# A perceiver block on one core: q turned through DRAM and by VectorE instead of by TensorE

## The reference, cut to what matters

```python
x = x + xattn(layernorm(x), ctx, ctx, 0, mask)   # 32 query heads of 32, 8 groups of keys (4 heads share one)
x = x + s4(layernorm(x))                         # along the 1024 features: a causal convolution with a kernel K, + D*u
x = x + ffn(layernorm(x))                        # 64 experts of rank 8, the best 16 of them by a router

def xattn(q, k, v, start, mask):                 # k = v = context
    scores = einsum('bsgrd,btgd->bgrst', xq, xk) / sqrt(32) + mask
    return einsum('bgrst,btgd->bsgrd', softmax(scores), xv)
```

## Time and profile before

| | |
|---|---|
| median of 3 runs | 1321.37 us |
| the profiled execution: its time, its span | 1324.92 us, 1323.1 us |
| TensorE busy, granted clock | 1270.4 us (96%), 0.991 |
| VectorE busy | 1132.9 us (86%) |
| ScalarE busy | 1057.1 us (80%) |
| GpSimd busy | 713.8 us (54%) |
| DMA | 132.87 MB, mean 100 GB/s |

### The profile page before, as it was taken

How to read it: one execution, slowest core, us unless ns; L and a number is a source line. 1 busy time by engine, 2 the same in 40 slices (tenths; PEclk the granted TensorE clock), 3 DMA queues, 4 the chain that set the end, 5 groups by cost and what they waited for, 6 DMA issues and landing times.

```text
span 1323.1 us, 42090 instructions
## 1 busy us (share of the span) xinstructions
PE 1270.4 (96%) x13932; PEld 1109.3 (84%) x13932; DVE 1132.9 (86%) x3656; ACT 1057.1 (80%) x3233; POOL 713.8 (54%) x939
## 2 busy tenths in 40 slices
PE   3679999999999999999999999999999999999997
PEld 2568888888888888888888888888888888888886
DVE  7988888888888898888888888888988888888853
ACT  2788888888888888888888888888888888888840
POOL 3346555665555566555556655555665555566320
PEclk9889999999999999999999999999999999999998
DMA  8343333443333344333334433343443334343210
GB/s 204 86 118 105 99 104 94 111 113 106 90 99 105 94 110 116 105 87 100 106 93 111 111 109 88 100 107 91 112 115 105 88 99 108 93 115 95 59 34 32
DMA packets 247896, 132.87 MB, mean 100 GB/s; under 512 B 192873, under 2 KB 234354, under 8 KB 247682
## 3 DMA queue, kind: packets, MB, share of 16 engines
q1 hardware_dynamic: 247682, 130.18, 36.8%
HBM read 111.72 MB, written 17.31 MB: 98 GB/s over the span
## 4 chain that ended last, share of the span: by engine, by line
PE 92%; DVE 3%; DMA 1%; ACT 1%; SPq 1%; issue 1%; DVEq 0%; ACTq 0%
PE ps_p L543 28%; PE ps_p L618 17%; PE ps_p L633 16%; PE ps_p L646 13%; PE ps_p L579 9%; PE ps_s L559 8%; ACT pr L807 1%; DMA tmp<-in_wide 1%; DVE ms L1337 0%; DVE x L1192 0%; DMA dn<-den 0%; SPq L381 0%; DMA kpad<-x 0%; DMA zg<-kpad 0%; DVE un L1251 0%
## 5 line engine op out<-in xcount | busy, mean ns | idle before, releaser
L807 ACT ACTIVATE pr<-ms,negmax 128x256 f32<-128x256 f32 x1024 | 515.0, 507 | 11.9 <-DVE negmax L1337 10.7
L1337 DVE CUSTOM_DVE_ANT_0 ms<-ps_s,neg_mask,last 128x256 f32<-128x256 f32 x1024 | 462.0, 471 | 50.0 <-PE ps_s L559 45.7
L759 ACT ACTIVATE pts<-ps_p 128x512 f32<-128x512 f32 x512 | 300.9, 596 | 151.2 <-PE ps_p L543 142.5
L543 PE MATMUL ps_p<-ident,pr 128*128 128x128 f32 x2048 | 311.4, 278 | 10.8 <-DVE wa_lo L1137 4.9
L543 PEld LDWEIGHTS ps_p<-ident,pr 128*128 128x128 f32 x2048 | 239.8, 141 | 50.4 <-issue 17.6
L1020 POOL TENSOR_TENSOR kt<-kr,kt 128x512 fp32r<-128x512 f32 x128 | 178.4, 1394 | 188.5 <-ACT kt L759 188.3
L807 ACT ACTIVATION_READ_ACCUMULATOR pr<-ms,negmax 128x1 f32 x1024 | 200.7, 196 | 0.0
L633 PE MATMUL ps_p<-wa_hi,ut_hi 128*128 128x288 f32 x512 | 160.2, 313 | 1.4 <-DVE ut_lo L1137 1.4
L618 PE MATMUL ps_p<-strip_hi,ut_hi 128*128 128x512 f32 (+2 forms) x384 | 151.8, 395 | 0.0
L633 PE MATMUL ps_p<-wa_lo,ut_hi 128*128 128x288 f32 x512 | 151.6, 296 | 0.0
L633 PE MATMUL ps_p<-wa_hi,ut_lo 128*128 128x288 f32 x512 | 151.5, 296 | 0.0
(11 more groups left out here) (139 smaller groups left out, 2715.6 us busy)
## 6 DMA issues: line engine op xcount, KB each, us to landing
kx<-in_ctx SPq DMA_DIRECT2D x512, 64.0 KB, 2.3
cx<-in_ctx SPq DMA_DIRECT2D x128, 256.0 KB, 2.9
xq<-in_x SPq DMA_DIRECT2D x32, 512.0 KB, 4.7
xr<-in_x SPq DMA_DIRECT2D x32, 512.0 KB, 3.7
out_x<-tmp SPq DMA_DIRECT2D x32, 512.0 KB, 3.9
dn<-den SPq DMA_DIRECT2D x512, 2.0 KB, 2.1
vl<-in_ctx SPq DMA_DIRECT2D x128, 32.0 KB, 1.8
last<-turn SPq DMA_DIRECT2D x128, 4.0 KB, 1.8
```

Source lines behind the costliest of these rows:

```text
L543: mm = pe.transpose(into[:, j * P:(j + 1) * P], source, ident[:, :])
L759: return act.activation(out, in_, ACT.Copy, scale=scale)
L807: act.activation(pr[:, b % 2, g, :], ms[:, n % MS, :], ACT.Exp, bias=negmax[:, n % MS:n % MS + 1], scale=-1.0, accum_out=den[:, b, g:g + 1 ...
L1337: dve.tensor_tensor_reduce(ms[:, n % MS, :], ps_s[:, g % GPH, g // GPH * SW:(g // GPH + 1) * SW], neg_mask[:, 0:SW], 1.0, last[:, it % 2, ...
```

## The change

q goes the keys' way. `q_norm` normalises x in place (in `xq`); SyncE stores `xq` to DRAM (`store_q`, 512 KB) and fetches it with four DMAs, one for each quadrant of 32 partitions (`move_q`, 128 KB each) into `qx`. VectorE's `q_turn(tile, h)` turns one half of it in 32x32 blocks into `qr`; `q_high` copies from `qr`, and `q_low` is now on GpSimd. `q_chunk` and its two banks go. As `qr` holds one half, `q_turn` of half 1 waits for `q_low` of half 0. As `lastp` holds one half too, GpSimd makes the product, the sums and the mask of the last row once for each half. `load_x` of the next tile waits until `last_product` has read xq. All queues and `BANKS` have a new order.

```diff
     "pair": ...
-    "q": (3, 0,),
-    "out": (1, 3,),
+    "out": (0, 0,),
...
-        qn = sb("qn", [P, HALVES, REP, P])
+        qx = sb("qx", [P, BPT, HALVES, REP, HEAD_DIM])
+        qr = sb("qr", [P, BPT, REP, SEQ])
...
             def load_x(tile):
+                if at(tile, 16, 0) > 0:
+                    sp.wait_ge(q_stored, at(tile, 16, 0))
                 if at(tile, 2, 0) > 0:
-                    sp.wait_ge(xq_used, at(tile, 2, 0))
+                    sp.wait_ge(lp_done, at(tile, 2, 0))
                 sp.dma_start(xq[:], rows(x_rows, tile)).then_inc(x_loaded, 16)
+            def store_q(tile):
+                sp.wait_ge(xq_used, at(tile, 2, 2))
+                if at(tile, 64, 0) > 0:
+                    sp.wait_ge(q_moved, at(tile, 64, 0))
+                sp.dma_start(turn_q.rearrange("b s c -> (b s) c"), xq[:, :]).then_inc(q_stored, 16)
+            def move_q(tile):
+                sp.wait_ge(q_stored, at(tile, 16, 16))
+                if at(tile, 2, 0) > 0:
+                    sp.wait_ge(qr_done, at(tile, 2, 0))
+                for quad in range(GPH):
+                    sp.dma_start(qx[SEQ * quad:SEQ * (quad + 1), :, :, :, :].rearrange("p b h r d -> p b (h r d)"),
+                                 turn_q.rearrange("b s (q c) -> s b q c", q=GPH)[:, :, quad, :]).then_inc(q_moved, 16)
...
-            def q_chunk(tile, h):
-                pe.wait_ge(xq_used, at(tile, 2, h + 1))
-                transposes([qn[:, h, r, :] for r in range(REP)], "q", h, tile, qt_done, ql_done, at(tile, 2, h + 1))
...
             def q_high(tile, h):
-                act.wait_ge(qt_done, at(tile, 2, h + 1))
+                act.wait_ge(qr_done, at(tile, 2, h + 1))
...
+            def q_low(tile, h):                      # on GpSimd, was on VectorE from the PSUM bank
+                pool.wait_ge(qh_done, at(tile, 2, h + 1))
+                pool.tensor_tensor(qs[:, tile % 2, 1, :, h, :, :], qr[:, :, :, :], qs[:, tile % 2, 0, :, h, :, :].bitcast(F32),
+                                   ALU.subtract).then_inc(ql_done, 1)
...
+            def q_turn(tile, h):
+                dve.wait_ge(q_moved, at(tile, 64, 64))
+                dve.wait_ge(ql_done, at(tile, 2, h))
+                dve.transpose(qr[:].rearrange("p b r s -> p b (r s)"),
+                              qx[:, :, h, :, :].rearrange("p b r d -> p b (r d)")).then_inc(qr_done, 1)
```

More of the change, by code:

```diff
@@ L457, in _ @@
[L457 to L461, removed]
+            load_s4(); load_x(0); load_mask(); load_last(0); load_router(); load_weight(0); load_keys(0, 0)
@@ L733, in _ @@
-            pair_chunk(1, 6); q_chunk(2, 1); attend(1, 0); attend(1, 1); pair_chunk(1, 7); scores(1, 3)
-            pair_chunk(1, 8); u_chunk(0, 0); attend(1, 2); attend(1, 3); pair_chunk(1, 9); u_chunk(0, 1)
-            convolve(0, 0, 0, 4); pair_chunk(1, 10); convolve(0, 1, 0, 8); pair_chunk(1, 11); z_chunk(0, 0, 0)
-            z_chunk(0, 1, 0)
+                if on(it - 2):
+                    expand(it - 2, 1, 1, 3)
+                pair_chunk(it, 11)
+                if on(it - 2):
+                    expand(it - 2, 1, 3, 4)
@@ L753, in _ @@
-            gated_chunk(31); expand(31, 0, 0, 4); expand(31, 1, 0, 4)
+            scores(31, 0); experts(29, 1, 0, 4); pair_chunk(30, 12); experts(29, 1, 4, 8); pair_chunk(30, 13)
+            attend(30, 4); attend(30, 5); pair_chunk(30, 14); pair_chunk(30, 15); scores(31, 1)
+            attend(30, 6); attend(30, 7); pair_chunk(31, 0); experts(29, 0, 0, 3); out_chunk(30, 0)
+            pair_chunk(31, 1); experts(29, 0, 3, 5); out_chunk(30, 1); experts(29, 0, 5, 7); pair_chunk(31, 2)
+            experts(29, 0, 7, 8); pair_chunk(31, 3); scores(31, 2); gated_chunk(29); pair_chunk(31, 4)
@@ new lines, in _ @@
+            pair_chunk(31, 5); attend(31, 0); attend(31, 1); expand(29, 0, 0, 2); u_chunk(30, 0)
+            expand(29, 0, 2, 4); u_chunk(30, 1); pair_chunk(31, 6); convolve(30, 0, 0, 4); pair_chunk(31, 7)
+            pair_chunk(31, 8); scores(31, 3); pair_chunk(31, 9); convolve(30, 1, 0, 3); pair_chunk(31, 10)
+            convolve(30, 1, 3, 8); expand(29, 1, 0, 1); z_chunk(30, 0, 0); attend(31, 2); attend(31, 3)
+            z_chunk(30, 1, 0); expand(29, 1, 1, 3); pair_chunk(31, 11); expand(29, 1, 3, 4); experts(30, 1, 0, 4)
@@ new lines, in _ @@
+            pair_chunk(31, 12); experts(30, 1, 4, 8); pair_chunk(31, 13); attend(31, 4); attend(31, 5)
+            pair_chunk(31, 14); pair_chunk(31, 15); attend(31, 6); attend(31, 7); experts(30, 0, 0, 3)
+            out_chunk(31, 0); experts(30, 0, 3, 5); out_chunk(31, 1); experts(30, 0, 5, 8); gated_chunk(30)
+            expand(30, 0, 0, 2); u_chunk(31, 0); expand(30, 0, 2, 4); u_chunk(31, 1); convolve(31, 0, 0, 4)
+            convolve(31, 1, 0, 8); expand(30, 1, 0, 1); z_chunk(31, 0, 1); z_chunk(31, 1, 1); expand(30, 1, 1, 4)
@@ L755, in _ @@
+            experts(31, 1, 0, 8); experts(31, 0, 0, 8); gated_chunk(31); expand(31, 0, 0, 4); expand(31, 1, 0, 4)
         @block.scalar
@@ L1091, in iteration @@
                 if on(it + 1):
-                    row_scale(0, it + 1)
-                k_low(it, 3)
+                    k_low(it + 1, 0)
                 last_shift(it, 0)
@@ new lines, in _ @@
+            k_low(0, 3); last_product(1, 0); last_shift(0, 0); k_low(1, 0); last_sum(1, 0); last_mask(1, 0)
+            last_product(1, 1); k_low(1, 1); last_shift(0, 1); last_sum(1, 1); last_mask(1, 1); k_low(1, 2)
+            last_shift(0, 2); q_low(1, 0); k_low(1, 3); q_low(1, 1); last_shift(0, 3); k_low(2, 0); row_scale(0, 2)
+            last_shift(1, 0); last_share(0, 0); residual(0, 0); last_share(0, 1); residual(0, 1); last_shift(1, 1)
+            first_residual(0, 0); k_low(2, 1); first_residual(0, 1); last_product(2, 0); row_scale(1, 0)
```

643 lines of the change are left out of this document (314 added, 329 removed).

## The result

The changed kernel takes 1326.9 us (median of four runs, 1326.67 to 1329.45) against 1321.46 us for four runs of the kernel before, made beside it: ratio 1.004, 95% interval 1.0023 to 1.0056. So it is slower by 0.4%, where I had forecast 1306 us and given "slower" one chance in ten. The profiled execution took 1327.04 us with a span of 1325.2.

A forecast was written before the change was run, and what follows sets the result against it. TensorE, busy 96%, was taken as the bound. Per tile -0.88 + 0.25 + 0.28 - 0.15 = -0.50 us, -14.5 us in all, with head and tail -0.5, gave a median of 1306 us; 8 in 10 range 1290 to 1321.

The forecast's parts named there:

- What goes from TensorE: TensorE's queue in the steady part: the two q_chunks' transposes go, -0.88 us a tile (0.80 to 0.88).
- What comes on the other engines: VectorE +0.06 us a tile, 90% busy and not the bound; GpSimd 26.5 us of 38; q's way through DRAM covered.
- (b): After scores 2: VectorE's row_norm waits for GpSimd's last_product on the shared port, delaying u_chunk 0, +0.28 us a tile.
- Rival 2: Gain mostly given back: VectorE runs late between scores 1 and 2, leaving 0 to 0.2 us a tile, 1315 to 1321; chance 0.18.
- Step 9 of the routing: Between maximum 8 and out_half 0 on VectorE: steps 8 and 9 (0.58 us) leave, step 4 (0.14) comes.
- (a): After scores 1: one bank for both halves of "out", so TensorE's out_chunk 1 waits for out_half 0, +0.25 us a tile.
- The 0.15 that I gave gated_chunk: gated_chunk starts 0.74 us behind an out_chunk where 0.44 would do; half of the 0.30 taken, -0.15 us a tile.
- Head and tail: Outside the steady tiles: head +1.5 us for q's store and fetch, tail -2 as expand products fill TensorE's wait; together -0.5.
- Rivals 3 and 4: x lands late and stops TensorE (1335); q's block transposes cost twice the keys' (1316); over 1322, chance 0.15 in all.

The follow-up runs named there:

- b_q2: Kernel before, with each q_chunk's four transposes made twice into the same bank: 1345.2 us, ratio 1.0164.
- a_k: Changed kernel, with the first k_low of a tile waiting on GpSimd until both q_norms are done: 1312.4 us, ratio 0.9924.
- b_two: Kernel before, with routing step 9 as a tensor_scalar with one tensor operand and the second last_product behind row_norm: 1323.4 us, ratio 1.0008.
- a_kr: Changed kernel, with the first k_low behind both q_norms and routing step 9 with one tensor operand: 1301.5 us, ratio 0.9845.
- a_three: Changed kernel, first k_low behind both q_norms, first last_product behind row_norm, routing step 9 with one tensor operand: 1301.5 us, ratio 0.984.
- a_k1: Changed kernel, with the first k_low of a tile waiting behind the first q_norm only: 1313.6 us, ratio 0.9938.

## Why the prediction was wrong, by its own steps

**What goes from TensorE, -0.88 a tile: right.** 0.84 by `b_q2`. The difference of the repaired kernels is 0.81, but this has the late denominators of seven tiles in it, so it isn't a second measurement of the same term.

**The failed step is "What comes on the other engines".** I wrote there that q_norm in place "has the same elements", so +0.06 us a tile for all of VectorE, and at (b) that q_low "meets no tensor_scalar of VectorE's". Both hold, and they are not the question. I priced VectorE's operations at the durations of the old schedule, and checked against GpSimd only one (row_norm) and only GpSimd's new operation. The new order has both q_norms in one piece, and GpSimd, behind the row_scale that they wait for and one row_scale more, goes on with k_low(., 0) just as they start. The same thing as (b), in a second place: 0.9 us a tile, which TensorE feels as 0.59 in the tile of the table and 0.45 over 28 tiles. Rival 2 had it in half a sentence, "q_norm there may start under k_low ... and cost up to 0.8"; it came to 0.9 for the pair, and I gave that rival 0.18. It looked for q_norm between scores 1 and 2; the pair runs between scores 0 and 1, and its delay comes through. Even then I took 0 to 0.2 us a tile as left, and the change cost 0.05.

**Step 9 of the routing was in no sum but as an item of 0.58 us with step 8**, that leaves the stretch before out_half 0, at its price in the kernel before, where it took 0.40 on average. It has two SBUF operands and now starts just behind first_residual's start, each time: 1.00 us, in front of out_half 1, and pair 3, which got the bank of "out" too, waits for that (0.34 us a tile). The prediction named only out_chunk 1 as waiting for this one bank.

**(a), +0.25: right in kind and too small, 0.47.** TensorE came to it 5.27 us behind scores 1 (5.30 forecast) and started at 5.74 (5.55 forecast). But with the q_norms free the wait is gone from most tiles (`a_k`): out_half 0 then comes 3.34 us behind maximum 8, where I had counted 3.68. My count held steps 6 and 7 at what they took in the kernel before, 0.66 and 0.79 on average; in `a_k` the tile has 0.23 and 0.93. So the 0.25 was there only because other operations were late, and that its sign came true is in part luck. **(b), +0.28: right in kind and too big**, 0.15 to 0.16; row_norm took 1.67 (I said 1.8). The 0.15 that I gave gated_chunk was read from one odd tile: in the trace of before gated_chunk starts 0.44 us behind the out_chunk in every steady tile but the one shown in the earlier trace rows.

So the forecast of -0.50 misses the measured +0.05 by 0.55. The terms that the runs took apart make more than that: pair 3 +0.34, the wait between scores 0 and 1 +0.12, (a) +0.22, (b) -0.13, the transposes +0.04, gated_chunk +0.15, together +0.74. So 0.19 us a tile went that no term of mine has. The repaired kernel says the same: a tile without late denominators takes 7.22 + 7.88 + 10.48 + 11.91 = 37.49 us, 1.0 less than the 38.51 of `b_two`, where `b_q2` gives 0.84 for the transposes. Where this comes from stays open.

**Head and tail.** Head 0 for +1.5. Tail +0.85 for -2: the wait for the split is gone as I said, yet another came before it. The chain of the changed kernel in the tail, in order of time, has GpSimd's work for tile 31 (the last row's share, L1096, and the residuals, L1105 and L1101), for which TensorE waits:

```profile
1281.01 1.09 POOL tmp L1096
1282.10 0.07 issue
1282.16 1.28 POOL tmp L1105
1283.45 1.05 POOL tmp L1096
1284.49 0.03 issue
1284.56 1.28 POOL tmp L1105
...
1287.02 1.28 POOL x L1101
...
1289.87 2.93 PE ps_p L665 x6
```

I didn't try an edit of the tail, so this is read and not shown by a run. The same chain comes to GpSimd from the denominators' way through DRAM (3.40 us from 1276.51), of which the prediction said nothing.

**Rivals 3 and 4: dead.** Of the 64 q_turns the mean is 0.705 us, no wait of VectorE for q's way stands in the trace, and only two for x, both in the head (0.5 us at 7 and 1.3 us at 111).

**The rule of the skill** that I leaned on for (b), Trainium skill (SBUF — State Buffer, SBUF: two separate sides), also says that a VectorE operation with two SBUF inputs contends with GpSimd's reads. The rows agree, with 1.00 us against 0.20 for one column. Had I held the whole rule against every VectorE operation between scores 0 and scores 2, and not against one, it would have pointed at both misses: at the q_norms as at row_norm, and at step 9 by its two inputs.

## What to carry to other kernels

When an edit moves work between queues, price every two-input or normalising operation of VectorE anew against what GpSimd runs at that time in the new order, and not by its mean of before (and read a price from several tiles, not from one); a product of two 128x1 columns can cost 1 us. If VectorE turns out late, look for such a pair first: one wait that lets VectorE go first, or one operand less, was worth 13 to 15 us here, while moving TensorE's work around the wait was worth nothing. The version to keep is `a_kr` (or `a_three`): 1301.5 us, 1.6% faster than the kernel before. What holds it up next, in seven of 27 tiles of `a_three`, are the denominators that land late.

## What the runs showed of the hardware

- A tensor_scalar of VectorE on 128x512 (0.54 us alone) or 128x1024 (0.81) that starts during a GpSimd tensor_tensor gets little done until that ends: a pair that takes 0.99 us took 1.91 and ended 0.73 behind it; row_norm ended 0.55 behind it and took 1.67.
- In these runs the one that started first was not disturbed and the other paid. GpSimd paid in `a_k1`, 1.47 us for 1.29.
- A small operation isn't spared: 128x1 with two SBUF tensors took 0.99 to 1.01 us in each of 27 tiles. With one tensor and the other factor as a scalar through a pointer it took 0.20 in the middle of a GpSimd operation. Why a tensor_scalar of one column runs through and one of 512 columns does not, no run here takes apart.
- 17 MB more of DRAM to DRAM traffic (183 MB in 1328 us) showed in no time.
